# Edge rows without a ones column: 2 KB pieces per partition, and the degrees by one-column products of their own

## The reference

```python
N, E = 3125, 103125                     # dst is sorted
deg = segment_sum(ones(E), dst, N)      # edges that end in a node
agg = segment_sum(edge_attr_64, dst, N) # N x 64
x = layernorm(x + gcn(x, ...))          # scaled by rsqrt(max(deg, 1))
x = layernorm(x + gru(x, ...))          # mean over incoming and outgoing edges
x = layernorm(x + mlp([x, agg, u]))     # three matrix products
x = layernorm(x + sage(x, ...))         # mean over incoming edges
```

## Time and profile before

| | |
|---|---|
| three runs, median (lowest to highest) | 847.89 us (846.87 to 848.69) |
| the profiled execution, its own time | 847.82 us |
| its span (first to last instruction) | 846.2 us |
| busy in the span: PE, DVE, ACT, POOL | 723.7, 609.8, 339.1, 21.7 us |
| DMA bytes, packets | 43.04 MB, 161,337 |
| packets under 512 B | 155,080 |

### The profile page before, as it was taken

One profiled execution on the slowest core, in us unless ns is written; L12 is line 12 of the kernel. 1 busy time (PEld: TensorE's weight loads), 2 busy tenths in 40 slices (PEclk: granted clock), 3 DMA queues, 4 the chain that ended last, 5 costly groups with the idle time before them and its releaser, 6 DMA issues.

```text
span 846.2 us, 16643 instructions
## 1 busy us (share of the span) xinstructions
PE 723.7 (86%) x6585; PEld 632.2 (75%) x6585; DVE 609.8 (72%) x974; ACT 339.1 (40%) x643; POOL 21.7 (3%) x41
## 2 busy tenths in 40 slices
PE   5476767676759999999989999969979999999995
PEld 2365656565659999799989997535548999699994
DVE  6999999999957777777777874758576554045554
ACT  0245555555555322422354233255325323332233
POOL 3500000000000000000000000000000000000000
PEclk9569999999997999999999999989998999999997
DMA  4457788877852000000000000000000000000001
GB/s 99 113 113 166 161 178 177 185 171 175 174 107 59 1 1 1 2 1 1 1 21 1 1 1 3 0 4 10 1 0 26 0 0 1 1 1 1 1 25 53
DMA packets 161337, 43.04 MB, mean 51 GB/s; under 512 B 155080, under 2 KB 159761, under 8 KB 161189
## 3 DMA queue, kind: packets, MB, share of 16 engines
q1 hardware_dynamic: 148042, 39.81, 21.0%
q10 hardware_dynamic: 11932, 0.81, 0.9%
q0 software_dynamic: 1280, 1.29, 0.6%
HBM read 39.07 MB, written 2.01 MB: 49 GB/s over the span
## 4 chain that ended last, share of the span: by engine, by line
PE 70%; DVE 12%; issue 7%; SPq 6%; DMA 2%; ACT 2%; POOL 0%; DVEq 0%; ACTq 0%
PE bank L1729 21%; PE bank L1730 21%; PE bank L1648 6%; PE bank L1660 3%; SPq L556 3%; PE bank L1937 2%; PE bank L1945 2%; PE bank L1633 2%; SPq L558 2%; PE bank L1791 1%; SPq L553 1%; PE bank L1988 1%; PE bank L1989 1%; PE bank L1742 1%; PE bank L1804 1%
## 5 line engine op out<-in xcount | busy, mean ns | idle before, releaser
L1729 PE MATMUL bank<-stage,f_hi 125*128 125x392 f32 x1000 | 348.6, 349 | 2.2 <-issue 2.2
L1730 PE MATMUL bank<-stage,f_lo 125*128 125x392 f32 x1000 | 342.3, 342 | 0.0
L1136 DVE CAST stage<-counts 125x2352 fp32r<-125x2352 uint8 x120 | 164.3, 1380 | 81.1 <-PE bank L1730 80.9
L797 ACT ACTIVATE stage<-counts 125x1568 fp32r<-125x1568 uint8 x80 | 108.1, 1351 | 227.9 <-PE bank L1730 224.4
L1729 PEld LDWEIGHTS bank<-stage,f_hi 125*128 125x128 f32 x1000 | 189.9, 190 | 3.5 <-issue 2.4
L1730 PEld LDWEIGHTS bank<-stage,f_lo 125*128 125x128 f32 x1000 | 189.7, 190 | 0.6
L1648 PE MATMUL bank<-rowb,xT 128*128 128x125 bf16 x1250 | 88.2, 227 | 65.9 <-issue 58.9
L1648 PEld LDWEIGHTS bank<-rowb,xT 128*128 128x128 bf16 x1250 | 78.4, 101 | 70.9 <-issue 70.9
L750 ACT ACTIVATE counts<-bank 125x500 uint8<-125x500 f32 x188 | 87.4, 538 | 94.5 <-PE bank L1648 93.8
L1069 DVE TENSOR_TENSOR xT<-xT,tmp 128x2560 bf16<-128x2560 bf16 (+1 forms) x63 | 92.6, 1470 | 0.0
L1072 DVE TENSOR_TENSOR rowb<-xT,rowb 128x2500 bf16<-128x2500 bf16 (+1 forms) x63 | 90.7, 1440 | 0.0
(11 more groups left out here) (228 smaller groups left out, 725.7 us busy)
## 6 DMA issues: line engine op xcount, KB each, us to landing
wb<-in_edge_attr SPq DMA_DIRECT2D x125, 256.0 KB, 4.0
wa<-in_x SPq DMA_DIRECT2D x12, 125.0 KB
out<-wl SPq DMA_DIRECT2D x6, 250.0 KB
xT<-in_dst SPq DMA_DIRECT2D x63, 4.0 KB, 3.5
xT<-in_dst ACTq DMA_DIRECT2D x62, 4.0 KB, 3.1
eaT<-eaT SPq DMA_DIRECT2D x1, 784.0 KB, 6.6
wb<-in_L_gnn_w_ih SPq DMA_DIRECT2D x1, 384.0 KB, 3.3
gate_w_d<-wl SPq DMA_DIRECT2D x1, 384.0 KB, 3.4
```

What stands on the lines that cost most here:

```text
L797: nc.scalar.activation(set_buffer(u, m), counts[:, SETS[u][0]:sum(SETS[u]), chunk(c)], ACT.Copy).then_inc(s["set_a_ready"], 1)
L1136: nc.vector.tensor_copy(set_buffer(u, m), counts[:, SETS[u][0]:sum(SETS[u]), chunk(pair * 2 + off)]).then_inc(s["set_d_ready"], 1)
L1729: mm(bank[h][:, 0:CH], f_hi[:, first + k, :], rhs[:, k, :], start=(first + k == 0), stop=False)
L1730: last = mm(bank[h][:, 0:CH], f_lo[:, first + k, :], rhs[:, k, :], start=False, stop=(first + k == HI - 1))
```

## The change

The edge rows are kept with a pitch of 64 instead of 66: the eight rows of a partition are now one run of 2 KB (512 numbers) in SBUF. The ones columns go. Instead POOL writes one single column of ones, `one_f`, into wb behind the six buffers. The edge product has 64 moving columns instead of 65, and after the eight products of an edge block come eight more with the same weights and `one_f` as the only moving column. They write the same column 64 of the block's part of the PSUM bank as before, and the last of them, not the last feature product, now raises `ea_made`.

```diff
-        ea_in = [wb[:, r * TE * 66:(r + 1) * TE * 66].rearrange("p (j f) -> p j f", j=TE) for r in range(RE)]
+        one_f = wb[:, 6 * TE * DE:6 * TE * DE + 1]
+        ea_in = [wb[:, r * TE * DE:(r + 1) * TE * DE].rearrange("p (j f) -> p j f", j=TE) for r in range(RE)]
...
-                sp.dma_start(ea_in[e % RE][:, :, 0:DE], edge_attr[bass.ds(first, ECAP), :].rearrange("(p j) c -> p j c", j=TE)).then_inc(ea_ready[e % RE], 16)
+                sp.dma_start(ea_in[e % RE], edge_attr[bass.ds(first, ECAP), :].rearrange("(p j) c -> p j c", j=TE)).then_inc(ea_ready[e % RE], 16)
...
-            for r in range(RE):
-                last = nc.gpsimd.memset(ea_in[r][:, :, DE:DE + 1], 1.0)
-            last.then_inc(s["slots_clean"], 1)
+            nc.gpsimd.memset(one_f, 1.0).then_inc(s["slots_clean"], 1)
...
-                        last = mm(bank[5 + r][quad:quad + 32, k * (DE + 1):(k + 1) * (DE + 1)], oh_dst_row[r][:, at:at + 32], ea_in[e % RE][:, j, 0:DE + 1],
-                                  start=(j < 4), stop=(j >= 4))
+                        mm(bank[5 + r][quad:quad + 32, k * (DE + 1):k * (DE + 1) + DE], oh_dst_row[r][:, at:at + 32], ea_in[e % RE][:, j, :], start=(j < 4), stop=(j >= 4))
+                    for j in range(TE):
+                        quad = 32 * (j % 4)
+                        at = (k * TE + j) * EW
+                        last = mm(bank[5 + r][quad:quad + 32, k * (DE + 1) + DE:(k + 1) * (DE + 1)], oh_dst_row[r][:, at:at + 32], one_f, start=(j < 4), stop=(j >= 4))
                     last.then_inc(s["ea_made"], 1)
```

## The result

The changed kernel takes 851.27 us (median of 12 runs, 849.05 to 851.79), the kernel before, beside it, 847.13 us (12 runs, 846.15 to 849.0). The ratio is 1.0036, with a 95% interval of 1.0025 to 1.0047: slower, by some 3 us by the ratio and 4.1 between the medians, where no change was forecast. Its profiled execution took 849.06 us with a span of 847.3, against 847.82 and 846.2; it is among the fastest of its 12 runs, so its profile holds only a part of the loss.

The account below looks back on a forecast made before the run. DVE's three instructions per group were taken to bound the loop. From the profiled 847.82 us, +0.3 at the loop's end, -0.25 in the loop and 0 elsewhere gave 847.87, predicted as 847.9 us, range 846.1 to 849.8.

Parts of the forecast that it names:

- The bound of the loop: Loop over 63 groups: DVE's three instructions set the 3.258 us period; PE has 0.98 us to spare in each group.
- The one-column products: Loop: 16 more products per group cost PE 0.3 us, bounds 0.21 to 0.59.
- Four records per 27 ns: Added products: four strips overlap, so a record costs 6.7 ns, 0.21 us a group, the lower bound.
- What hides it: Loop: DVE's period covers the added products, up to 30.6 ns a record.
- that close to being late: Loop: only 0.26 us in all are lost to anything but DVE's own work; edge loads are no closer to late.
- So inside the loop nothing moves: Loop: `ea_made` up to 0.15 us later per block, 0.3 at the upper price, delays nothing that matters.
- The loads: Loop: edge loads in 2 KB pieces lower the DMA share to about 0.6 and gain 0.25 us (0 to 0.26).
- The end of the loop: Groups 61 and 62 through the write of the degrees: no cover, so +0.3 us, bounds +0.2 to +0.9.
- 0 elsewhere: Sum: everything outside the loop and its end, the start included, was counted as no change.
- the signs that the prediction named as right: Period 3.258 us, PE wait about 0.7, records 7 to 18 ns apart, DMA share near 0.6, degrees written near 245.5.
- Rival 2: After the loop: a 0.3 us later start shifts the clock; up to 852 or 845.4 us; chance 0.07 slower, 0.05 faster.
- The range's lower end: Whole kernel: the forecast's own lower bound, 846.7 us, widened by half the runs' spread and part of Rival 2 to 846.1.

Follow-up runs that it names:

- e1: Kernel before, 256-byte loads kept, plus eight more one-column products per block whose sums nobody reads: 859.21 us, ratio 1.0102.
- e12: Kernel before with eight unread one-column products per block, 256-byte loads kept, and 96 idle PE instructions: 852.84 us, ratio 1.0062.
- e6: Kernel before with 160 idle instructions on PE in the loop, so later code lies as in the changed kernel: 849.95 us, ratio 1.0032.
- e2: Changed kernel's pitch and loads with the old number of products, reading a fixed buffer of ones: 847.76 us, ratio 0.9982 against the kernel before.
- e5: Changed kernel with 96 idle PE instructions, so code after the loop lies as in the kernel before: 847.33 us, ratio 1.0005 against the kernel before.
- e8: The changed kernel run again unaltered in the second session, against the kernel before: 849.76 us, ratio 1.0040.
- e13: Changed kernel with 68 idle PE instructions, against the kernel before: 847.24 us, ratio 0.9995.
- e0: The changed kernel once more, unaltered, for a second profile, against the kernel before: 850.57 us, ratio 1.0012.
- e7: Changed kernel with its one-column products in bf16 and 48 idle instructions for the placement of before: 847.46 us, ratio 1.0011 against the kernel before.
- e9: Kernel before with 256 idle PE instructions, one whole piece of code: 850.93 us, ratio 1.0026.
- e14: Changed kernel with 64 idle PE instructions, run a second time, against the kernel before: 852.91 us, ratio 1.0067.
- e15: Kernel before with 224 idle PE instructions, code around the branch lying as in the changed kernel with 64: 854.28 us, ratio 1.0083.
- e3: Kernel before with unread one-column products in the last two groups alone (96 instructions): 851.66 us, ratio 1.0028.
- e10: Changed kernel with 64 idle PE instructions, first run, against the kernel before: 853.72 us, ratio 1.0065.
- e11: Changed kernel with 160 idle PE instructions, against the kernel before: 848.27 us, ratio 0.9996.

## Why the prediction was wrong

**The bound of the loop: right.** DVE's period stayed 3.258 us, PE's spare time shrank from 0.98 to 0.76.

**The one-column products: right, at the lower end.** 0.22 us a group, of 0.21 to 0.59, 0.3 taken. "Four records per 27 ns" is what the trace shows, 7 ns. By the Trainium skill, "TensorEngine Tiling (Array Packing)", Instruction Overhead, one moving column takes as long as 60, which gave an estimate of 0.54 us. For 32 weight columns in four column strips the trace doesn't agree: 0.22.

**What hides it: right for this kernel, with a reason that was missing.** The prediction took the products and the loads one by one, and for each found that nothing waits. e1 and e12 show that they are not independent: with the loads of before the same products cost over 5 us of loop, and DVE waits for the load of dst, which stands behind the edge load in SP's queue. Whether the products' 0.2 us or the stops for code make it late is open. The earlier trace rows had the warning, two waits for an edge load, and the prediction itself wrote that the loads are "that close to being late". "So inside the loop nothing moves" is true only together with the new loads (they land in 3.1 us instead of 4.0 in the median).

**The loads: inside the bounds, but not shown by the profiles.** -0.25 us, of 0 to -0.26, is a difference of two single profiles. The loop takes 182.41 us in e6 too, and there the loads are those of before; such a difference can come by itself. Over many runs the loads alone gain 0.2% (e2, 0.9982).

**The end of the loop: right within its bounds.** From line 1648 of group 61 to SP's write of the degrees it was 4.27 us and is 4.48, +0.21, of +0.2 to +0.9; 0.3 taken. Other profiles bear this out: from the start of group 62's first one-hot to that write are 3.96 to 4.01 us without the products (before, e2, e6) and 4.17 to 4.23 with them (changed, e5, e8, e13), though 4.91 in e0. By line 1104 it is +0.17, less than that way differs from run to run.

**The step that failed is "0 elsewhere" in the sum.** It counted the 4,000 added instructions as work on PE and not as a length. They move all later code by 15.6 pieces, and the code of before happens to have neither of the two bad positions at the branch. What stood at 0 measured 0.4 to 0.9 us more of waiting at the branch and 0.3 to 1.5 us behind it, and some 3 us in the ratio. All the signs that the prediction named as right came (the period, 0.76 us, 7 ns, a share of 0.64, the write of the degrees 0.4 us from where it said); they stood in the place of the edit, and none looked behind 268 us. Rival 2 had part of it: a start somewhat later tips the granted clock. But it looked only at the stretch behind the loop, which kept its length (253.5 to 263.7 us before, 253.9 to 264.1 now), and gave it 0.12 in all. A rival of some weight was missing: that the moved code changes the wait at the branch and what the clock does behind it. The trace of before had the place, though not the price: 0.93 us of PE waiting at 523.39 with DVE done, and a branch record of 3.77 us. The range's upper end, 849.8, left it out. The range's lower end has a slip of its own: 846.7 less half the spread of the runs (0.9) is 845.8, not 846.1; nothing hangs on it here.

The Trainium skill has the rule, in "Runtime: NRT & Kernel Launch", Instruction fetch mechanics: instructions stream in blocks of 16 KiB, crossing a boundary is mostly hidden, and a taken branch whose target isn't in the two blocks held has to load it first. This trace agrees on the packets and on the stall, some 3.3 to 4.5 us here. That a crossing is hidden does not hold just before a branch and just behind its target. In straight code it holds in the profiles of the kernel before, e2, e5, e6, e7, e9, e14, e15 and the first of the changed kernel; in eight others PE stops in the middle of groups, each time until 1.2 to 1.7 us after a packet has landed: once in e3 and e10, twice in e8, three to five times in e0, e11 and e13, ten times in e12, 16 times in e1.

**What stays open.** How the 0.4 to 0.9 us at the branch become the 3 us of the ratio. In the profiled executions much of the rest is in half-clock stretches: a longer one at 561 us in the changed kernel and in e8 (but not in e0), an additional one between 522 and 531 us in e3, e6, e10, e14 and e15. That the longer wait brings them is not shown; no run holds the clock and moves the code alone. Also open are the 2.8 us of e9's loop, and why code comes late in e1's and e12's loops and not in that of the changed kernel's first profile. No kernel that ran beats the kernel before with the whole computation: e5, e11 and e13, the changed kernel well placed, are equal to it.

## What to carry over

A change that adds or removes instructions moves all code behind it; where the program branches later, that is a cost or gain of its own, of up to 7 us here (e15), and it says nothing about the idea. Compare such a change with its code brought to the same place by idle instructions before judging it (a few of them: e9, with 256, lost 0.26% in the loop), and look at the waits called "issue" behind branches first. And when two edits of one change touch the two ends of one chain (who frees a buffer, how long its load takes), price them together: one of them may be paying for the other. And profile a run whose own time is near the median: the first profile of the changed kernel was one of its two fastest runs, and shows about a third of the loss.

## What the runs showed of the hardware

- Instructions come in packets of 16,384 bytes, 64 bytes per instruction, each taking 0.9 to 2.1 us. In the kernel before 26 of them come from 58 to 246 us, and PE stops for none. In e1's loop, with more instructions in a group and edge loads in 256-byte pieces as before, PE stops 16 times for 0.6 to 2.0 us, and each stop ends 1.3 to 1.6 us after a packet has landed; e12 has ten such stops.
- PE's sequencer ran some 3 us ahead of its products at the branch (branch at 519.35, last product's result used by DVE until 522.46). That hides most of the branch's 3.29 to 3.77 us. Where a piece was entered just before the branch, it took 3.98 to 4.48 us. A further packet began 0.7 to 1.2 us after the branch's end; with a boundary right behind the target PE stood for another 2.7 to 3.5 us (e10, e14, e15).
- One-column fp32 products with 32 weight columns in four column strips: 7 ns a record. In bf16, half as many records, the whole kernel's time was the same (e7 847.46 us, e5 847.33).
- DMA pieces of 2 KB in place of 256 bytes: the share of the 16 engines in the loop falls from 0.82 to 0.64 at nearly the same bytes, and a load of 256 KB lands in 3.1 us instead of 4.0.
